# Running maxima of the edge attention passes: scans on 32 rows of 128 slots in place of 1024 slots on four partitions

## What is computed

```python
amax = jax.ops.segment_max(alpha, dst, num_segments=n)
expa = jnp.exp(alpha - amax[dst])
denom = jax.ops.segment_sum(expa, dst, num_segments=n)
attn = expa / (denom[dst] + 1e-16)
out = jax.ops.segment_sum(attn[:, :, None] * v_j, dst, num_segments=n)
```

## Time and profile before

| | |
|---|---|
| median of 3 runs | 13408.96 us (13392.93 to 13420.43) |
| span of the profiled execution, first to last instruction | 13400.0 us |
| PE busy | 8527.8 us (64%) |
| DVE busy | 10400.3 us (78%) |
| ACT busy | 3614.6 us (27%) |
| POOL busy | 6926.8 us (52%) |

### The profile page before, as it was taken

How to read it: one execution, slowest core, us unless ns; L and a number is a source line. 1 busy time by engine, 2 the same in 40 slices (tenths; PEclk the granted TensorE clock), 3 DMA queues, 4 the chain that set the end, 5 groups by cost and what they waited for, 6 DMA issues and landing times. The chain is left out here.

```text
span 13400.0 us, 212567 instructions
## 1 busy us (share of the span) xinstructions
PE 8527.8 (64%) x52858; PEld 6962.8 (52%) x52859; DVE 10400.3 (78%) x15015; ACT 3614.6 (27%) x7819; POOL 6926.8 (52%) x7047
## 2 busy tenths in 40 slices
PE   4663477776777677775465652777266666567764
PEld 3553245554455535654455542555266666566664
DVE  8666569974799748996688875888778888688888
ACT  0111133332333233332244431333211111111111
POOL 2775047750477407772277750777145555255553
PEclk8555688877888788887688875666588888788887
DMA  4334754444544474443255550222233334233333
GB/s 182 113 113 119 244 206 106 106 80 193 192 106 106 72 292 123 106 106 53 79 145 145 146 111 19 55 55 54 19 103 106 107 107 105 75 108 105 105 106 72
DMA packets 720185, 1523.62 MB, mean 114 GB/s; under 512 B 364796, under 2 KB 416585, under 8 KB 680627
## 3 DMA queue, kind: packets, MB, share of 16 engines
q0 software_dynamic: 306624, 795.04, 25.0%
q1 hardware_dynamic: 413427, 727.07, 15.9%
HBM read 1050.48 MB, written 471.10 MB: 114 GB/s over the span
## 5 line engine op out<-in xcount | busy, mean ns | idle before, releaser
L970 POOL DMA_INDIRECT h<-table,edges_ring x3984 | 3856.5, 968 | 1889.0 <-issue 1154.3
L1147 PE MATMUL bank<-h,edges_onehot 128*128 128x260 f32 (+1 forms) x7968 | 1986.6, 406 | 652.3 <-issue 469.0
L1147 PEld LDWEIGHTS bank<-h,edges_onehot 128*128 128x128 f32 x7968 | 1570.6, 246 | 978.1 <-issue 717.4
L970 POOL DMA_INDIRECT edges_rows<-table,edges_ring x1512 | 1527.0, 1010 | 716.0 <-issue 431.0
L1122 PE MATMUL bank<-ident,edges_score 128*4 128x128 f32 x5280 | 1027.7, 360 | 1021.5 <-DVE edges_score L1288 737.9
L1258 DVE TENSOR_TENSOR_SCAN bank<-edges_fresh,edges_top,bank 4x1024 f32<-4x1024 bf16 x660 | 1541.5, 2336 | 144.9 <-PE bank L1122 141.2
L1265 DVE TENSOR_TENSOR_SCAN edges_top<-edges_fresh,bank 4x1024 f32<-4x1024 bf16 x660 | 1493.8, 2263 | 0.6 <-issue 0.3
L1122 PEld LDWEIGHTS bank<-ident,edges_score 128*4 128x4 f32 x5280 | 497.6, 104 | 1339.0 <-DVE edges_score L1288 784.9
L1314 DVE TENSOR_TENSOR acc<-acc,bank 128x260 f32 (+1 forms) x2640 | 908.9, 344 | 164.4 <-PE bank L1147 60.4
L2017 POOL DMA_INDIRECT rec<-dst,slots x782 | 797.0, 1019 | 432.7 <-issue 432.4
L1203 ACT ACTIVATE edges_onehotT<-bank 128x1024 bf16<-128x1024 bf16 (+1 forms) x550 | 562.1, 1022 | 1153.3 <-PE bank L1087 715.9
(11 more groups left out here) (346 smaller groups left out, 18152.3 us busy)
## 6 DMA issues: line engine op xcount, KB each, us to landing
table<-x SPq DMA_DIRECT2D x154, 1040.0 KB, 7.9
edge_score<-edge_feat SPq DMA_DIRECT2D x220, 512.0 KB, 3.8
table<-h SPq DMA_DIRECT2D x77, 1040.0 KB, 7.9
table<-source_typed_rows SPq DMA_DIRECT2D x63, 1040.0 KB, 8.1
h<-table,edges_ring POOLq DMA_INDIRECT x3984
edge_feat<-edge_score SPq DMA_DIRECT2D x110, 512.0 KB, 2.9
dst_row<-dst_rows SPq DMA_DIRECT2D x71, 704.0 KB, 4.2
buf<-rec SPq DMA_DIRECT2D x44, 840.0 KB, 5.2
```

The source lines that it names most:

```text
L970: pool.indirect_dma_start(out=rows[s % R][:, j, :], out_offset=None, in_=table, in_offset=bass.IndirectOffsetOnAxis(ap=ring[:, s * ST + j: ...
L1147: ins = pe.matmul(sum_b[k % 3], onehot[s][:, j, :], rows[s][:, j, A0:W], start=j == k * GT, stop=j == (k + 1) * GT - 1)
```

## The change

Scores are turned in one transpose to 32 partitions, one for each head and tile (RUNS = 32), of 128 slots. The mark of a run's begin is loaded in that form, 32 rows of 385 marks, with a second, short transfer of 64 marks (`line`). `find_ends` (DVE) reduces for each row the maximum of the run that is still open at its end and of the run that is open at its begin. `line_up` (PE) puts these 64 numbers, and the last running maximum of the superblock before, side by side on one partition. `link` (DVE) scans them, 32 up and 32 down. `turn_line` (PE) turns the result to the 32 rows, where it is the start value of each, and `scan_both` (DVE) scans 128 slots up and 128 down. `turn_top` turns 32 rows back in one transpose and forms the rise of the maximum by two products, of which ACT takes Relu before Exp. The fall's own DVE instruction is gone. DVE reads all four bin numbers at the head of its step. Ahead of the passes one block makes the marks in their new form, and a few small constants (`pick`, `head_first`, `head_last`).

```diff
@@ attention_edges, buffers and banks
-        score = [p.buffer(f"score{s}", (P, ST, HEADS)) for s in range(2)]
-        fresh = [p.buffer(f"fresh{s}", (HEADS, SLOTS_SB + 1), BF16) for s in range(2)]
-        top = [p.buffer(f"top{s}", (HEADS, SLOTS_SB)) for s in range(2)]
-        fall = p.buffer("fall", (HEADS, 1))
+        score = [p.buffer(f"score{s}", (P, HEADS, ST)) for s in range(2)]
+        marks = [p.buffer(f"marks{s}", (RUNS, MARKS), BF16) for s in range(2)]
+        line = [p.buffer(f"line{s}", (1, LINE)) for s in range(2)]
+        ends, masked = p.buffer("ends", (RUNS, 2)), p.buffer("masked", (RUNS, 2, P))
+        linked = p.buffer("linked", (1, LINE + 1))
+        rising = [p.buffer(f"rising{s}", (RUNS, P)) for s in range(2)]
+        top, drop = p.buffer("top", (RUNS, P)), p.buffer("drop", (P, HEADS))
@@ SP
-                    sp.dma_start(fresh[s][:, :], g.fresh_d[bass.ds(u * SLOTS_SB, SLOTS_SB + 1)].partition_broadcast(HEADS)
+                    sp.dma_start(marks[s][:, :], g.marks_d[bass.ds(u, 1), :, :].rearrange("u r c -> (u r) c")
                                  ).then_inc(fresh_in[s], 16)
+                    sp.dma_start(line[s][:, :], g.lines_d[bass.ds(u, 1), :]).then_inc(fresh_in[s], 16)
@@ PE
-                    for j in range(ST):
-                        ins = pe.transpose(score_b[0:HEADS, j * P:(j + 1) * P], score[s][:, j, :], g.ident[:, :])
-                    ins.then_inc(score_turned, 1)
+                    pe.transpose(score_b, score[s][:, :, :].rearrange("p h t -> p (h t)"), g.ident[:, :]
+                                 ).then_inc(score_turned, 1)
+                def line_up(m):
+                    u, s = number(m), m[1] % 2
+                    pe.wait_ge(ends_found, u + 1)
+                    for k, last in enumerate((ends[:, 0:1], ends[:, 1:2], rising[1 - s][:, P - 1:P])):
+                        ins = pe.matmul(line_b, last, g.pick[0:RUNS, k, :], start=k == 0, stop=k == 2)
+                    ins.then_inc(line_made, 1)
+                def turn_line(m):
+                    pe.wait_ge(linked_made, number(m) + 1)
+                    pe.matmul(init_b[:, 0:1], linked[:, 0:RUNS], g.ones[0:1, 0:1], start=True, stop=True)
+                    pe.matmul(init_b[:, 1:2], linked[:, RUNS + 1:LINE + 1], g.ones[0:1, 0:1], start=True, stop=True
+                              ).then_inc(init_made, 1)
@@ PE turn_top
-                    pe.wait_ge(fall_made, u + 1)
-                    for j in range(ST):
-                        pe.transpose(top_b[:, j * HEADS:(j + 1) * HEADS], top[s][:, j * P:(j + 1) * P],
-                                     g.ident[0:HEADS, 0:HEADS])
-                    pe.matmul(fall_b, fall[:, 0:1].to_broadcast([HEADS, P]), g.ident[0:HEADS, 0:HEADS],
-                              start=True, stop=True).then_inc(top_turned, 1)
+                    pe.wait_ge(top_made, u + 1)
+                    pe.transpose(top_b, top[:, :], g.ident[0:RUNS, 0:RUNS])
+                    pe.matmul(drop_b, top[:, 0:1].to_broadcast([RUNS, P]), g.head_first[0:RUNS, :], start=True, stop=False)
+                    pe.matmul(drop_b, rising[1 - s][:, P - 1:P].to_broadcast([RUNS, P]), g.head_last[0:RUNS, :],
+                              start=False, stop=True).then_inc(top_turned, 1)
@@ PE step
+                    if o:
+                        sum_group(o, 0)
+                    if m:
+                        line_up(m)
+                    if o:
+                        sum_group(o, 1)
+                    if m:
+                        turn_line(m)
                     if n and conv is not None:
                         flip_onehot(n)
                     if o:
-                        for k in range(GPS - 1):
-                            sum_group(o, k)
+                        sum_group(o, 2)
@@ ACT
-                        act.activation(rate[s % 2][:, :], fall_b, ACT.Exp).then_inc(rate_made, 1)
+                        act.activation(drop[:, :], drop_b, ACT.Relu).then_inc(drop_taken, 1)
+                        act.wait_ge(drop_taken, u + 1)
+                        act.activation(rate[s % 2][:, :], drop[:, :], ACT.Exp, scale=-1.0).then_inc(rate_made, 1)
@@ DVE: scan_up, scan_down and find_fall give way to find_ends, link and scan_both
+                    for k, at in enumerate((2 * P + 1, 0)):
+                        ins = v.tensor_tensor_reduce(masked[:, k, :], score_b, marks[s][:, at:at + P], 1.0, -BIG,
+                                                     ALU.add, ALU.max, ends[:, k:k + 1])
+                    ins.then_inc(ends_found, 1)
...
+                    v.wait_ge(line_made, u + 1)
+                    v.tensor_tensor_scan(linked[:, 0:RUNS], line[s][:, 0:RUNS], line_b[:, 0:RUNS], -BIG, ALU.add, ALU.max)
+                    v.tensor_tensor_scan(linked[:, LINE - 1:RUNS - 1:-1], line[s][:, :RUNS - 1:-1], line_b[:, :RUNS - 1:-1],
+                                         -BIG, ALU.add, ALU.max).then_inc(linked_made, 1)
...
+                    v.wait_ge(init_made, u + 1)
+                    v.tensor_tensor_scan(rising[s][:, :], marks[s][:, P:2 * P], score_b, init_b[:, 0:1], ALU.add, ALU.max
+                                         ).then_inc(rising_made, 1)
+                    v.tensor_tensor_scan(top[:, ::-1], marks[s][:, 2 * P:P:-1], rising[s][:, ::-1], init_b[:, 1:2],
                                          ALU.add, ALU.max).then_inc(top_made, 1)
@@ DVE step
+                    bins = load_bins(v, g, number(o)) if o else []
                     if m:
-                        scan_up(m)
+                        find_ends(m)
                     if o:
-                        bins = [load_bin(v, g, number(o), k) for k in range(2)]
                         add_sums(o, 0, bins)
                     if m:
-                        scan_down(m)
+                        link(m)
                     if o:
-                        bins += [load_bin(v, g, number(o), k) for k in range(2, GPS)]
                         add_sums(o, 1, bins)
                     if m:
-                        find_fall(m)
+                        scan_both(m)
```

143 lines of the change are left out of this document (100 added, 43 removed).

## The result

The changed kernel takes **15447.8 us**, the median of 4 runs (15444.53 to 15450.83), where the kernel before took 13406.11 (4 runs) beside it: 1.1525 times as long, 95% interval 1.1508 to 1.1542. The forecast was 14750 with a range of 13900 to 15700. The sign was right, and so was most of the mechanism; the rise was 1.5 times the forecast's, 2042 us and not 1345, most of the rest by TensorE's clock.

A forecast was written before the change was run, and what follows sets the result against it. POOL was taken to bound relational passes, a DVE-PE loop convolution. Rises of 627 (relational), 198 (edges2), 495 (convolution) and 25 us (marks) sum to 1345 on a 13400.0 span: 14745, with 9 for the median 14750; range 13900 to 15700.

The forecast's parts named there:

- What bounds the passes: Relational passes: POOL bounds at 9.9 us a superblock; the DVE-PE loop has 0.7 us of slack and grows to 11.9.
- Rival B: Relational and edges2 loops stay under POOL's 10.0 us, so only convolution passes pay: 13920 us; chance 0.11.
- rival D: Convolution loop is set by DVE, so 2.7 us of DVE work falls out of 220 superblocks: 12830 us; chance 0.05.
- DVE's work, 2.7 us less: Every superblock: 4.8 us of DVE work removed, 2.1 added; worth nothing in four passes, where DVE is not the bound.
- Loads that no operation covers: DVE's four register loads, 0.74 us each, stand uncovered ahead of find_ends, which starts at +2.2 in relational passes.
- Rival C: Register loads run ahead of waits; four passes keep POOL's pace, convolution pays 1.3 us: 13710 us; chance 0.07.
- zero: Origin of the forecast's offsets: when DVE can start what follows weigh_rows, 1.14 us after that starts in a relational superblock.
- PE's second sum group, 1.1: Relational pass: second sums run +3.4 to +4.5, turn_line is let go at +4.2, PE's loads start at about +4.4.
- Rival A: Gaps lower PE's clock: 3.2 us more per convolution superblock, 1.2 per relational loop, 15850 us; full or large part, chance 0.15.
- PE's loads ... done at +7.4: Relational pass: PE's four register loads end at +7.4, after the flip at +6.6, so fourth sums start at +7.5.
- Convolution, 2.25: Convolution passes: first spread_half starts at +6.45, against +4.0; each superblock 2.25 us longer, 495 us over 220.
- The marks, 25 us: Ahead of the passes: making marks and constants takes about 25 us, bounds 10 and 60.

The follow-up runs named there:

- e1: Changed kernel with DVE's register loads back in two pairs, behind the step's first and second DVE operations; 15037.72 us, 1.1206 times the kernel before.
- e4: Changed kernel plus six unused 128x128 PE products a superblock in relational and edges2 passes; 14823.31 us, 1.1047 times the kernel before.
- e12: Changed kernel with DVE's register loads back behind find_ends and link, and six extra PE products in relational and edges2 superblocks; 14710.47 us, 1.0978 times the kernel before.
- e8: Changed kernel plus one unused DVE scan of 1024 elements on four partitions per superblock, on a slower chip; 16291.4 us, 1.0706 times the kernel before.
- e2: Changed kernel with PE's four register loads moved to the head of its step, ahead of every wait; 15915.43 us, 1.186 times the kernel before.

## Why the prediction was right, and where its sizes were off

Offsets from the one-hot's start in the second relational pass, in us, means over some 95 superblocks, worked out from the start times of the records:

| | forecast | after | e1 | e4 | e12 |
|---|---|---|---|---|---|
| find_ends | 2.2 | 2.28 | 1.13 | 2.28 | 1.13 |
| link | 3.6 | 3.82 | 3.68 | 3.77 | 3.72 |
| turn_line | 4.2 | 5.68 | 4.83 | 4.63 | 4.35 |
| flip | | 7.87 | 6.95 | 5.88 | 5.54 |
| spread_dst | 8.5 | 10.15 | 9.27 | 8.77 | 8.54 |
| period | 11.9 | 13.65 | 12.63 | 11.97 | 11.73 |

- **What bounds the passes: right.** The loop through DVE and PE had about 0.7 us of slack under POOL's pace, used it up and took the bound over; POOL now waits for PE as well. Rival B (POOL still covers) and rival D (faster) are out.
- **DVE's work, 2.7 us less and worth nothing: right,** shown by the busy time and by e8.
- **Loads that no operation covers: right on DVE.** `find_ends` at +2.2 is within 0.1 us in the mean, and e1 took the 1.0 us back. Rival C, loads that run ahead of waits, is refuted by e2. In convolution passes `find_ends` came at +0.84 on the row (12317.05 behind a zero of 12316.21) and at +0.93 in the mean, forecast +0.9.
- **"PE's second sum group, 1.1 ... so turn_line is let go at +4.2 and PE's loads start at about +4.4": the step that failed.** Its durations were those of the higher clock. With the clock at 0.62 the second sums take 2.1 us and `turn_line`, queued behind them, starts at +5.7 (by its own durations, too, the forecast had it at +4.2, ahead of the end of the sums at +4.5); from there to the end of the flip it is 3.2 us for 1.9 in e4. The same step at 0.84 (e4) gives +4.6, and a period of 12.0. So the clock is worth 1.6 us x 330 = 530 us in relational passes (13.62 for 12.01) and 0.6 x 110 = 66 in edges2. The profile had told of it: the third of 3.4 us that the forecast took from the earlier trace rows is the mean of two paces, for by the start times of these twelve products they are 0.43 us apart up to 2306.00 and 0.22 from there on. Rival A priced 1.2 us for this loop, with a chance of 0.15, and the forecast set the clock's part to none while calling a part of it likely.
- **"PE's loads ... done at +7.4", later than the flip: right only at the higher clock.** There they show as 1.3 us of idle time (e4, e12); in the changed kernel itself the slower sums cover them. The forecast's wait for the loads and rival A's slower products, put on top of it, stand side by side in part: the slower PE hides the loads.
- **Convolution, 2.25 for 3.12.** In the 89 superblocks at the higher clock the first half starts 2.99 us later (5.48 to 8.47); everything behind it kept its pitch, as forecast. The period of these superblocks is 2.85 us longer, 0.6 over the forecast: `turn_line` comes 0.4 later in the mean, for the two groups of sums ahead of it took 1.25 us each for the 0.9 forecast, and the way from the flip to the half is 3.35 us in the mean (3.47 on the row, 12300.37 to 12303.84) for 3.05. The 19 others cost 1.87 more each, 0.33 a superblock. That is 132 + 72 us, for the 191 that the passes took over the forecast.
- **The marks, 25 us: 23.**
- **The range** was built right: its upper end took in near half of rival A, and that is where the result fell. The forecast's own sum, with no term for the clock, did not lead there. That e4's 12.0 meets its 11.9 so closely is in part luck: `turn_line` and `spread_dst` are 0.4 and 0.3 us late there, and what follows `spread_dst` is 0.2 shorter than forecast.

## What to carry to other kernels

Ahead of cutting work from an engine, ask what stands beside it: the two long scans were the cover under which DVE read four registers and PE kept its pieces close. A change that puts two engines into alternation is to be priced twice, once with each duration of TensorE's that the trace shows, since here a group of products of 1.1 us became one of 2.1 when gaps came to stand ahead of it; and costs that lie side by side are combined by the later of them, not by a sum.

## What the runs showed of the hardware

- **Extra TensorE work shortened the kernel.** Six products a superblock raised the granted clock from 0.62 to 0.84 (between the levels of 1.2 and 2.4 GHz) and took 624 us off. Where they stand decides: behind the second half of a convolution superblock they raised the clock to 0.81 and changed nothing in the first halves. The Trainium skill (TensorE: Matmul & The Clock Gate, HAM oscillation — how this bites in real kernels) describes a loop in which every burst of products begins at the lower clock after a wait. The trace agrees in part: the first halves of 19 of 108 convolution superblocks do, and with the flip moved ahead all of them; in relational passes the first sums do in 320 of 325 superblocks, and by the fourth a group takes 1.24 us and not 2.10.
- **Register loads don't run ahead of PE's queue at will.** A load's own record is 0.30 us, and one follows another at 0.74. In e2 the first starts 0.1 us after the transpose ahead of it, though that one waited 3.35 us. In the changed kernel it starts with the third sums and the flip still ahead of it, but not before `turn_line` has begun, 1.7 us after the last wait was over. What lets it go there is not shown; a limit to what may be queued is one possibility, and no run tested it.
- **Two kinds of superblock in one loop.** The convolution pass of the changed kernel has periods of 17.9 and 19.7 us, with no difference in the code between them; a mean over the pass hides it.
- **The kernel before takes 13.4, 15.2 or 15.7 ms, by the chip.** On the two slower chips waits of 2 to 5 us with releasers named "issue" or "remote" stand in single superblocks. Their cause was not looked for.
